# A spectral convolution and spline network: part of the mixing weights loaded among the images, the square root's table loaded in the forward block, the pairs' bias computed behind the first mixing units, and the small loads issued by ScalarE

## The chip, the cores and the metric

The kernel runs on one core of a Trainium2 chip. The metric is the device time of one execution in microseconds (us); lower is better. A core has TensorE (PE, matmuls; its weight loads are shown apart as PEld), VectorE (DVE), ScalarE (ACT), GpSimd (POOL) and SyncE (SP). DMAs are issued by SP, ACT or POOL, each on a queue of its own, and all of them are moved by the core's 16 DMA engines.

## The reference

```python
x: (16, 64, 128, 128) f32          # batch, channels, height, width
xn = group_norm(x)                 # 32 groups of 2 channels, no affine part
# spectral convolution: keep 16 x 16 modes of the lowest and of the highest rows
x_ft = rfft2(xn)
out_ft[:, :, :16, :16]  = einsum('bixy,ioxy->boxy', x_ft[:, :, :16, :16],  w1_r + 1j * w1_i)
out_ft[:, :, -16:, :16] = einsum('bixy,ioxy->boxy', x_ft[:, :, -16:, :16], w2_r + 1j * w2_i)
y = irfft2(out_ft) + conv1x1(xn, conv_w) + conv_b
# two KAN layers on the channels: silu(y) @ base.T + cubic B-splines(y) . (spline * scaler)
y = kan(kan(y, k1), k2)
out = x + gelu(y)
```

Each of w1_r, w1_i, w2_r, w2_i is (64, 64, 16, 16) f32, 4 MB.

## The kernel before

The program has four blocks, one after the other; at the end of a block every engine waits for the others (the branch rows with line 296 stand there).

**Forward block** (`forward`). For each of the 16 images, SP loads eight chunks (`load` inside `forward`, line 362) of 512 KB into `big[:, 0:2]`, which holds two images. PE multiplies two chunks at a time by the DFT table along the height (`h`, line 491: four such stretches per image, h0 to h3, the first needing chunks 0 and 1, the second 2 and 3, and so on), ACT copies the result out of PSUM (line 580), PE turns it (`turn`, line 501), ACT orders it (line 588), and PE does the transform along the width one image late (`w`, line 513). DVE takes the statistics of each chunk (line 430) and keeps the modes (line 421). Chunk k of image b+2 is loaded when PE and DVE are done with chunk k of image b (`next_image`). Image 0 comes first; then DVE's spline weights, which start as soon as eight small loads by POOL's queue (`natural_loaded`) are there, are turned by PE (line 563) while DVE goes on to the statistics; then the images 1 to 15. The last image is followed by the means and variances (lines 538 to 546 on PE, 444 to 455 on DVE). Behind the images' loads SP issues the mixing weights of group 0: w1_r into `big[:, 2]` (eight DMAs of 512 KB, line 160) and the first half of w1_i into `big[:, 3]` (four).

**Mixing block** (`statistics_and_mix`). SP at once loads the rest: the second half of w1_i (whose place held scratch of the forward block), and then w2_r and w2_i over the two images' places; these are 4 + 8 + 8 = 20 DMAs of 512 KB. Meanwhile ACT takes the square root of the variance (line 716), DVE makes the reciprocal `rs_c` (lines 750 to 754) and the pairs' means (757, 758), PE makes the pairs' bias (688), DVE copies it (764, 766), and then the mixing starts. It runs in four passes: group 0 real, group 0 imaginary, group 1 real, group 1 imaginary, each needing its own 4 MB of weights, each of 8 units x; for each unit DVE scales the modes (line 785) and PE does 32 matmuls (705). Behind the second and the fourth pass ACT copies each finished unit (726) and stores it by two DMAs (729). When all are stored, SP loads the modes for the inverse transform.

**Second half** (`second_half`): inverse transform along the height, and then 128 tiles of the inverse along the width, 1x1 convolution and two KAN layers. It fills the rest of the time and no line of the change touches it.

The lines that release PE's first work, before (549 is the head of PE's part):

```python
            pe.wait_ge(tables_loaded, 48)          # dft_h, the identity and dft_w, 16 each
            image(0, 0, 0, before=False)
            pe.wait_ge(mats_ready, 1)
```

## Time and profile before

| | |
|---|---|
| median of 3 runs | 3696.25 us (3695.16 to 3698.87) |
| the profiled execution | 3700.55 us, of which the span shown in the trace is 3698.7 us |
| PE busy | 3629.4 us, 98% of the span |
| DVE, ACT, POOL busy | 3480.8, 3374.5, 116.3 us |
| forward block | 0 to 248.7 us of the span |
| mixing block | 248.7 to about 332 us |
| second half | about 332 us to the end |

The trace shows one execution; times in it count from the start of its span. A row of a timeline has the start, the time from the first to the last instruction of the row, the engine, the line, the operation, the tiles written and read, the count, and in brackets how long the engine sat idle ahead of it and what released it. The DMA share in a window can stand above 1, because packets of one engine overlap.

### The profile page before, as it was taken

To read this page: it belongs to the slowest core of one execution; us is meant where nothing else is said; L and a number is where in the kernel's file an instruction comes from. 1 tells how busy PE (TensorE), PEld (TensorE's weight loads), DVE (VectorE), ACT (ScalarE), POOL (GpSimd) and SP (SyncE) were. 2 spreads that over 40 slices of the span, in tenths; PEclk is the share of its full clock that TensorE was granted. 3 is DMA by queue.
4 is the path that set the end of the run, shared out by engine and by line. 5 is a ranking of instruction groups with operands and counts; after the bars stand their busy time and mean duration, and the time that the engine had idled before them with its cause. 6 is when DMAs were issued, how large, how long until landed. Compare 5 with 4: busy or idle time off the path is not lost.

```text
span 3698.7 us, 98607 instructions
## 1 busy us (share of the span) xinstructions
PE 3629.4 (98%) x36932; PEld 1565.2 (42%) x36932; DVE 3480.8 (94%) x3548; ACT 3374.5 (91%) x3510; POOL 116.3 (3%) x140
## 2 busy tenths in 40 slices
PE   8987999999999999999999999999999999999998
PEld 4555657654333333333333333333333333333333
DVE  8875999999999999999999999999999999999997
ACT  4433999999999999999999999999999999999997
POOL 0000000000000000000000000000000000000000
PEclk9998999999999999999999999999999999999999
DMA  9998243432322323223232232322323222232231
GB/s 320 328 214 200 61 120 89 118 93 60 76 69 65 77 58 76 68 66 77 58 76 67 67 74 60 77 66 68 73 61 77 64 70 71 63 77 64 70 73 50
DMA packets 269760, 338.45 MB, mean 92 GB/s; under 512 B 83272, under 2 KB 198824, under 8 KB 267624
## 3 DMA queue, kind: packets, MB, share of 16 engines
q1 hardware_dynamic: 248392, 265.50, 25.3%
q0 software_dynamic: 18720, 67.49, 10.1%
q10 hardware_dynamic: 2560, 4.20, 0.4%
q8 instruction: 67, 1.10, 0.1%
q14 instruction: 21, 0.17, 0.0%
HBM read 248.50 MB, written 88.61 MB: 91 GB/s over the span
## 4 chain that ended last, share of the span: by engine, by line
PE 90%; SPq 1%; issue 1%; DMA 1%; ACTq 0%; ACT 0%; DVE 0%; DVEq 0%
PE l_ps L1241 84%; PE y_banks L1218 3%; PE y_banks L1227 2%; SPq L160 1%; PE y_banks L1260 1%; PE y_banks L1202 1%; PE y_banks L1189 0%; PE y_banks L1241 0%; DMA big<-in_spec_w_i_dram 0%; ACTq L729 0%; ACT mixed L726 0%; DMA rows_scratch<-rows 0%; PE l_ps L1260 0%; DMA modes_scratch<-mixed 0%; PE mix_ps L705 0%
## 5 line engine op out<-in xcount | busy, mean ns | idle before, releaser
L1121 ACT ACTIVATE offset<-size 128x1024 f32<-128x1024 f32 x1280 | 1241.0, 1045 | 8.1
L1047 DVE SCALAR_TENSOR_TENSOR cube0r<-below,offset 128x1024 f32<-128x1024 f32 x256 | 312.6, 1221 | 113.2 <-ACT offset L1121 103.2
L1047 DVE SCALAR_TENSOR_TENSOR cube2r<-below,offset 128x1024 f32<-128x1024 f32 x256 | 311.5, 1217 | 0.6 <-PE l_ps L1241 0.6
L1047 DVE SCALAR_TENSOR_TENSOR cube0l<-above,offset 128x1024 f32<-128x1024 f32 x256 | 311.7, 1217 | 0.0
L1047 DVE SCALAR_TENSOR_TENSOR cube1r<-below,offset 128x1024 f32<-128x1024 f32 x256 | 311.6, 1217 | 0.0
L1047 DVE SCALAR_TENSOR_TENSOR cube1l<-above,offset 128x1024 f32<-128x1024 f32 x256 | 311.6, 1217 | 0.0
L1047 DVE SCALAR_TENSOR_TENSOR cube3r<-below,offset 128x1024 f32<-128x1024 f32 x256 | 311.5, 1217 | 0.0
L1047 DVE SCALAR_TENSOR_TENSOR cube2l<-above,offset 128x1024 f32<-128x1024 f32 x256 | 311.5, 1217 | 0.0
L1047 DVE SCALAR_TENSOR_TENSOR cube3l<-above,offset 128x1024 f32<-128x1024 f32 x256 | 311.5, 1217 | 0.0
L1047 DVE SCALAR_TENSOR_TENSOR cube4l<-above,offset 128x1024 f32<-128x1024 f32 x256 | 311.4, 1217 | 0.0
L1047 DVE SCALAR_TENSOR_TENSOR cube4r<-below,offset 128x1024 f32<-128x1024 f32 x256 | 311.4, 1216 | 0.0
L1057 DVE SCALAR_TENSOR_TENSOR inner_cube<-below,square 128x1024 f32<-128x1024 f32 x256 | 311.4, 1216 | 0.0
L1241 PE MATMUL l_ps<-S,turned_w 64*64 64x512 f32 x2040 | 280.9, 604 | 10.9 <-issue 10.9
L1117 ACT ACTIVATE size<-below 128x1024 f32<-128x1024 f32 x256 | 270.9, 1058 | 8.1
L1241 PE MATMUL l_ps<-cube0l,turned_w 64*64 64x512 f32 x2040 | 275.5, 590 | 1.7 <-issue 1.7
L1241 PE MATMUL l_ps<-below,turned_w 64*64 64x512 f32 x2040 | 276.6, 593 | 0.4 <-issue 0.4
L1241 PE MATMUL l_ps<-cube2r,turned_w 64*64 64x512 f32 x2040 | 275.5, 589 | 0.5 <-issue 0.5
L1241 PE MATMUL l_ps<-inner_cube,turned_w 64*64 64x512 f32 x2040 | 275.8, 589 | 0.0
L1241 PE MATMUL l_ps<-cube0r,turned_w 64*64 64x512 f32 x2040 | 275.8, 592 | 0.0
L1241 PE MATMUL l_ps<-cube4l,turned_w 64*64 64x512 f32 x2040 | 275.4, 589 | 0.0
L1241 PE MATMUL l_ps<-bowl,turned_w 64*64 64x512 f32 x2040 | 275.4, 589 | 0.0
L1241 PE MATMUL l_ps<-cube4r,turned_w 64*64 64x512 f32 x2040 | 275.4, 589 | 0.0
(169 smaller groups left out, 5963.3 us busy)
## 6 DMA issues: line engine op xcount, KB each, us to landing
big<-in_x_dram SPq DMA_DIRECT2D x128, 512.0 KB, 8.3
x_ring<-in_x_dram SPq DMA_DIRECT2D x256, 256.0 KB, 4.6
out_dram<-act_out SPq DMA_DIRECT2D x128, 512.0 KB, 2.6
act_out<-in_x_dram POOLq DMA_DIRECT2D x127, 512.0 KB, 7.0
rows_t<-rows_scratch SPq DMA_DIRECT2D x512, 32.0 KB
rows_scratch<-rows SPq DMA_DIRECT2D x14, 1024.0 KB, 6.8
pair_t<-pair_scratch SPq DMA_DIRECT2D x128, 65.0 KB, 1.9
big<-in_spec_w_r_dram SPq DMA_DIRECT2D x16, 512.0 KB, 11.6
```

The costliest lines, as they stand in the source:

```text
L160: sp.dma_start(dst[half * C:(half + 1) * C, o0:o0 + MIX_O, :, :], src[:, o0:o0 + MIX_O, x0:x0 + SH, :]).then_inc(t["mix_loaded"][g][part], 16)
L1047: nc.vector.scalar_tensor_tensor(out=cube[q][side][:], in0=distance[own][:], scalar=EDGE - KNOTS[q], in1=offset[own][q][:], op0=ALU.min, o ...
L1057: nc.vector.scalar_tensor_tensor(out=inner_cube[:], in0=below[own][:], scalar=EDGE, in1=square[own][:], op0=ALU.subtract, op1=ALU.mult).th ...
L1117: nc.scalar.activation(size[own][:], below[own][:], ACT.Abs, bias=EDGE, scale=-1.0).then_inc(size_ready[layer], 1)
L1121: nc.scalar.activation(offset[own][q][:], size[own][:], ACT.Square, bias=-KNOTS[q]).then_inc(offset_ready[layer], 1)
L1202: ins = nc.tensor.matmul(y_ps[image, at:at + W], rows[half, par, h, :], inv_w_sb[half, i, :], start=False, stop=(h == HH - 1), skip_group_ ...
L1218: nc.tensor.matmul(y_banks[image, at:at + GW], pair_t[par][half, image], src[half, i * MM + g2 * GW:i * MM + (g2 + 1) * GW], start=True, s ...
L1227: ins = nc.tensor.matmul(y_banks[:, at:at + W], rows[q, par, 2 * e:2 * e + 2, :].rearrange("q i o -> q (i o)"), inv_w4_sb[q, :], start=Fal ...
L1241: ins = nc.tensor.matmul(dst[cols, r * MM:(r + 1) * MM], kan_w[layer][rows_, f, :], src[rows_, n * MM:(n + 1) * MM], start=(f == 0), stop= ...
L1260: ins = nc.tensor.matmul(inv_bank(n, u)[h], inv_h_sb[own, part, h], spec[pair % 2][own, cols:cols + MM], start=True, stop=True, tile_posit ...
```

## The change

Of w1_r, four of the 64 output channels are now loaded after each of the images 2 to 15, as two DMAs of 128 KB (14 times, 56 channels); the last eight channels and the first half of w1_i follow as before. PE's first work waits for the table along the height alone; the other two tables are waited for ahead of the first `turn`. The eight small loads move from POOL's queue to ACT's, ahead of everything else on ACT. A square root of one element, which is used by nobody, stands at the end of ACT's part of the forward block. In the mixing block the pairs' means, PE's bias and its copies move behind DVE's second and fourth unit and PE's second; the bias is written to the PSUM banks of the last two units instead of the third and fourth, and DVE's first pass is written out instead of looped.

```diff
+O_IMAGE = 4
+O_AMONG = O_IMAGE * (B - 2)
+def load_mix_weights_among(sp, t, dst, image):
+    for half in range(2):
+        x0 = SH * half
+        sp.dma_start(dst[half * C:(half + 1) * C, bass.ds((image - 2) * O_IMAGE, O_IMAGE), :, :],
+                     t["w1_r"][:, bass.ds((image - 2) * O_IMAGE, O_IMAGE), x0:x0 + SH, :]).then_inc(t["mix_loaded"][0][0], 16)
...
-            sp.dma_start(dft_h_sb[:], t["dft_h"]).then_inc(tables_loaded, 16)
+            sp.dma_start(dft_h_sb[:], t["dft_h"]).then_inc(dft_h_loaded, 16)
...
                 for par in range(2):
                     next_image(b2, par)
+                    sp.wait_ge(weights_turned, len(TURNS))
+                    load_mix_weights_among(sp, t, weights[:, 2], 2 * b2 + par)
             sp.wait_ge(consts_loaded, 160)
-            sp.wait_ge(weights_turned, len(TURNS))
-            load_mix_weights(sp, t, weights[:, 2], 0, 0, 0, C)
+            load_mix_weights(sp, t, weights[:, 2], 0, 0, O_AMONG, C)
             load_mix_weights(sp, t, weights[:, 3], 0, 1, 0, C // 2)
-        @block.gpsimd
-        def _(pool):
...
-                pool.dma_start(kan["spline"][own], s_).then_inc(natural_loaded, 16)
-                pool.dma_start(kan["scaler"][own], c_).then_inc(natural_loaded, 16)
-                pool.dma_start(kan["mats"][own, F_SILU, :], b_).then_inc(natural_loaded, 16)
-                pool.dma_start(kan["mats"][own, NF, :], t["conv_w"]).then_inc(natural_loaded, 16)
...
                 for k in range(1, N_GRP // 2):
                     h(b, b2, par, k)
+                    if k == 1 and not before:
+                        pe.wait_ge(tables_loaded, 32)
...
-            pe.wait_ge(tables_loaded, 48)
+            pe.wait_ge(dft_h_loaded, 16)
...
+                nc.scalar.dma_start(kan["spline"][own], s_).then_inc(natural_loaded, 16)
+                nc.scalar.dma_start(kan["scaler"][own], c_).then_inc(natural_loaded, 16)
+                nc.scalar.dma_start(kan["mats"][own, F_SILU, :], b_).then_inc(natural_loaded, 16)
+                nc.scalar.dma_start(kan["mats"][own, NF, :], t["conv_w"]).then_inc(natural_loaded, 16)
             act.sem_inc(flat_ready, 4)
             act.sem_inc(freq_ready, 2)
             image(0, 0)
...
+            act.wait_ge(averages_set, 2)
+            nc.scalar.activation(root_of_one, avg[:, 0:1], ACT.Sqrt)
...
-        ps_bias = [ps[2 + i][:, 0:PAIRS] for i in range(2)]
+        ps_bias = [ps[SH - 2 + i][:, 0:PAIRS] for i in range(2)]
...
-                    pe.wait_ge(t["mix_loaded"][g][part], 32 * (C // MIX_O))
+                    pe.wait_ge(t["mix_loaded"][g][part], 32 * (C // MIX_O if g + part else B - 1))
...
+                        if g == 0 and part == 0 and x == 2:
+                            bias()
+                        if g == 0 and part == 0 and x == SH - 2:
+                            pe.wait_ge(bias_kept, 1)
...
+            for x2 in range(SH // 2):
+                for u in range(2):
+                    norm(0, 0, x2, u)
+                if x2 == 0:
+                    means_of_pairs()
+                if x2 == 1:
+                    bias_of_pairs()
```

How it stands on the queues, in the order of each engine's instructions. First SP, from the end of its loop over the images on: `in_x_dram` are the images, `in_spec_w_r_dram` w1_r (and, in the mixing block, w2_r), `in_spec_w_i_dram` w1_i (and w2_i); REGISTER_ALU and COMPARE_AND_BRANCH end the loop, and the two UNCONDITIONAL_BRANCH rows are the way from the forward block to the mixing block. Before:

```order
L362 ISA
L362 DMA big<-in_x_dram 128x4x256
L395 REGISTER_ALU
L395 COMPARE_AND_BRANCH
L160 DMA big<-in_spec_w_r_dram 64x16x128 x8
L160 DMA big<-in_spec_w_i_dram 64x16x128 x4
L296 UNCONDITIONAL_BRANCH
L661 UNCONDITIONAL_BRANCH
L160 DMA big<-in_spec_w_i_dram 64x16x128 x4
L160 DMA big<-in_spec_w_r_dram 64x16x128 x8
L160 DMA big<-in_spec_w_i_dram 64x16x128 x8
```

The same place now (the loop's body, for two images, ends with the first six rows; the pair of weight DMAs stands behind the first image of the body too, and the last w_i row, x8, follows the last row shown):

```order
L160 ISA x2
L160 DMA big<-in_spec_w_r_dram 64x4x128
L160 ISA
L160 DMA big<-in_spec_w_r_dram 64x4x128
L409 REGISTER_ALU
L409 COMPARE_AND_BRANCH
L173 DMA big<-in_spec_w_r_dram 64x8x128 x2
L173 DMA big<-in_spec_w_i_dram 64x16x128 x4
L309 UNCONDITIONAL_BRANCH
L677 UNCONDITIONAL_BRANCH
L173 DMA big<-in_spec_w_i_dram 64x16x128 x4
L173 DMA big<-in_spec_w_r_dram 64x16x128 x8
```

Eight DMAs of 512 KB ahead of the branch have become 28 of 128 KB inside the loop and two of 256 KB behind it; what stands behind the branch is the same twenty as before.

Then ACT at the start of the program, first before and then now (`flat_or_spec<-along_h` is the copy that waits for PE's first stretch, `in_k_...` and `in_conv_w_dram` are the small loads):

```order
L575 UNCONDITIONAL_BRANCH
L580 ACT_TABLE_LOAD
L580 ACTIVATE flat_or_spec<-along_h 128x512 x2
L588 ACTIVATE freq<-planes 128x33x8
L580 ACTIVATE flat_or_spec<-along_h 128x512
```

```order
L582 UNCONDITIONAL_BRANCH
L607 DMA big<-in_k_spline_dram 64x512
L608 DMA big<-in_k_scaler_dram 64x64
L609 DMA big<-in_k_base_dram 64x64
L610 DMA big<-in_conv_w_dram 64x64
L607 DMA big<-in_k_spline_dram 64x512
L608 DMA big<-in_k_scaler_dram 64x64
L609 DMA big<-in_k_base_dram 64x64
L610 DMA big<-in_conv_w_dram 64x64
L587 ACT_TABLE_LOAD
L587 ACTIVATE flat_or_spec<-along_h 128x512 x2
```

Eight DMA issues now stand ahead of ACT's first work, and ahead of its increments of `flat_ready`, for which PE's first stretch waits.

Last, ACT from the end of its loop over the images to its first copy of a mixed unit, first before and then now (`root<-var` is the root that DVE waits for):

```order
L605 COMPARE_AND_BRANCH
L296 UNCONDITIONAL_BRANCH
L713 UNCONDITIONAL_BRANCH
L716 ACT_TABLE_LOAD
L716 ACTIVATE root<-var 128x16
L726 ACTIVATE mixed<-mix_ps 128x512
```

```order
L619 COMPARE_AND_BRANCH
L623 ACT_TABLE_LOAD
L623 ACTIVATE big<-big 128x1
L309 UNCONDITIONAL_BRANCH
L734 UNCONDITIONAL_BRANCH
L737 ACTIVATE root<-var 128x16
L747 ACTIVATE mixed<-mix_ps 128x512
```

The table load has moved from behind the branch to ahead of it, with one more small ACTIVATE.

## Rows read from the trace of the kernel before

**Rows 1.** The page: its span, and the chain that ended last, by engine

```profile
span 3698.7 us, 98607 instructions
...
PE 90%; SPq 1%; issue 1%; DMA 1%; ACTq 0%; ACT 0%; DVE 0%; DVEq 0%
```

**Rows 2.** Windows: length, busy us (instructions) by engine, PEclk, DMA share, GB/s

```profile
40.00:140.00 100.00, 100.00 (x1252) 57.67 (x1254) 87.35 (x259) 49.96 (x117) 0.00 (x0) 1.00 1.09 348
140.00:205.00 65.00, 65.00 (x776) 36.12 (x769) 55.79 (x166) 33.03 (x78) 0.00 (x0) 1.00 0.97 312
210.00:215.00 5.00, 5.00 (x48) 2.44 (x42) 5.00 (x16) 2.64 (x8) 0.00 (x0) 1.00 1.23 184
240.00:249.00 9.00, 6.77 (x52) 2.66 (x46) 5.78 (x11) 0.28 (x1) 0.00 (x0) 1.00 0.46 70
249.00:312.00 63.00, 44.73 (x772) 43.25 (x772) 38.86 (x85) 6.02 (x10) 0.56 (x1) 0.85 1.14 214
```

**Rows 3.** Timeline of PE: first stretches of images 1, 2, 15; last of 2

```profile
29.40 3.66 PE L491 MATMUL along_h<-big,dft_h_sb 64*64 64x512 f32 x32 [1.16 <-ACT turned_w L602]
...
43.10 3.66 PE L491 MATMUL along_h<-big,dft_h_sb 64*64 64x512 f32 x32
...
50.62 1.95 PE L491 MATMUL along_h<-big,dft_h_sb 64*64 64x512 f32 x16
...
221.11 3.66 PE L491 MATMUL along_h<-big,dft_h_sb 64*64 64x512 f32 x32
```

**Rows 4.** Timeline of SP in the forward block, two of its rows

```profile
32.25 172.81 SPq L362 DMA_DIRECT2D big<-in_x_dram  x112
205.31 19.52 SPq L160 DMA_DIRECT2D big<-in_spec_w_r_dram  x8
```

**Rows 5.** Line 362, image loads, from 30 to 62 us

```profile
DMA to landing us min/median/max: 3.9/8.6/9.0
```

**Rows 6.** Waits on SP, from 140 to 180 us: total, times, longest

```profile
SPq L390 <- PE along_h L491: 15.1, 9, 4.3
```

**Rows 7.** Line 160, weight loads, from 249 to 312 us; issue ns min/median/max

```profile
L160 SPq DMA_DIRECT2D big<-in_spec_w_i_dram x12: 595/2654/4190, 248.7 to 300.9; - x12
L160 SPq DMA_DIRECT2D big<-in_spec_w_r_dram x8: 2712/2949/3614, 254.1 to 275.3; - x8
...
DMA to landing us min/median/max: 5.8/12.4/13.1
```

**Rows 8.** Timelines of PE, PEld, DVE at the start of the program

```profile
9.33 6.01 PE L491 MATMUL along_h<-big,dft_h_sb 64*64 64x512 f32 x32 [9.33 <-DMA dft_w_sb<-dft_w_dram]
...
11.06 0.28 PEld L491 LDWEIGHTS along_h<-big,dft_h_sb 64*64 64x64 f32 x4 [0.57 <-issue]
13.10 0.33 PEld L491 LDWEIGHTS along_h<-big,dft_h_sb 64*64 64x64 f32 x8 [1.76 <-issue]
...
11.94 0.69 DVE L241 TENSOR_TENSOR big<-big 128x512 f32<-128x512 f32 x1 [9.58 <-DMA big<-in_conv_w_dram]
...
24.72 3.53 PE L563 MATMUL planes<-eye_all,big 128*64 128x128 f32 x60 [0.58 <-ACT freq L588]
```

**Rows 9.** Timeline of ACT: DMA issues beside SP's full queue

```profile
276.91 1.10 ACTq L729 DMA_DIRECT2D modes_scratch<-mixed  x2
...
290.86 1.94 ACTq L729 DMA_DIRECT2D modes_scratch<-mixed  x2
```

**Rows 10.** Timelines of ACT, DVE and PE in the mixing block

```profile
248.72 1.28 ACT L716 ACT_TABLE_LOAD   x1 [9.80 <-PEq L296]
...
251.47 0.16 DVE L757 COPY pair_mean<-mean_c 64x8 f32<-64x8 f32 x1
...
253.46 0.16 DVE L769 COPY rs_own<-rs_c 64x16 f32<-64x16 f32 x1
...
255.95 14.52 PE L705 MATMUL mix_ps<-big,stats 128*64 128x64 f32 x256 [3.23 <-DVE stats L785]
...
312.05 14.52 PE L705 MATMUL mix_ps<-big,stats 128*64 128x64 f32 x256 [6.95 <-DMA big<-in_spec_w_i_dram]
```

More of the change, by code:

```diff
@@ L157, in load_mix_weights @@
     for o0 in range(o_first, o_end, MIX_O):
+        o1 = min(o0 + MIX_O, o_end)
         for half in range(2):
             x0 = SH * (half if g == 0 else 1 - half)
-            sp.dma_start(dst[half * C:(half + 1) * C, o0:o0 + MIX_O, :, :],
-                         src[:, o0:o0 + MIX_O, x0:x0 + SH, :]).then_inc(t["mix_loaded"][g][part], 16)
+            sp.dma_start(dst[half * C:(half + 1) * C, o0:o1, :, :],
+                         src[:, o0:o1, x0:x0 + SH, :]).then_inc(t["mix_loaded"][g][part], 16)
 def place(j):
@@ L326, in forward @@
             for k in range(3))
+        root_of_one = late[:, at + 7 * n_bg:at + 7 * n_bg + 1]
         flat = [t["flat_or_spec"][:, i * HALF * W:(i + 1) * HALF * W].rearrange("p (f w) -> p f w", w=W) for i in range(2)]
@@ L340, in forward @@
         img_loaded = [[sem(f"img_loaded{p}{k}") for k in range(N_GRP)] for p in range(2)]
-        tables_loaded = sem("tables_loaded")
+        tables_loaded, dft_h_loaded = sem("tables_loaded"), sem("dft_h_loaded")
         along_h_done, flat_ready = sem("along_h_done"), sem("flat_ready")
@@ L684, in _, with bias @@
         def _(pe):
-            pe.wait_ge(rm_ready, 1)
-            for i in range(2):
-                rows = slice(i * C, (i + 1) * C)
-                ins = nc.tensor.matmul(ps_bias[i][rows, :], conv_two[rows], pair_rm[rows, :], start=True, stop=True,
-                                       tile_position=(i * C, i * C))
-            ins.then_inc(bias_done, 1)
+            def bias():
+                pe.wait_ge(rm_ready, 1)
+                for i in range(2):
+                    rows = slice(i * C, (i + 1) * C)
+                    ins = nc.tensor.matmul(ps_bias[i][rows, :], conv_two[rows], pair_rm[rows, :], start=True, stop=True,
+                                           tile_position=(i * C, i * C))
+                ins.then_inc(bias_done, 1)
             pe.sem_inc(mix_done, 2)
@@ L773, in _ @@
                                                 op0=ALU.mult, op1=ALU.add))
-            for g in range(2):
-                for pass_ in range(2):
-                    with dve.Fori(0, SH // 2) as x2:
-                        for u in range(2):
-                            place_ = 2 * x2 + u if g == 0 else x2 * -2 + (SH - u)
-                            dve.wait_ge(mix_done, 2 * x2 + (2 * SH * g + SH * pass_ + u + 1))
-                            here = modes[:, bass.ds(place_, 1), g, :, :].rearrange("p s (k r) b -> p (s k) r b", r=2)
-                            takes = ((0, rs_own), (1, rs_own)) if pass_ == 0 else ((1, rs_neg), (0, rs_own))
-                            for f, (part, scale) in enumerate(takes):
-                                ins = nc.vector.tensor_tensor(
-                                    normed[u][:, :, f, :, :], here[:, :, part:part + 1, :].to_broadcast([P, MODES, 2, B]),
-                                    scale[:].unsqueeze(1).to_broadcast([P, MODES, 2, B]), ALU.mult)
-                            ins.then_inc(normed_ready, 1)
-                    if g == 0 and pass_ == 0:
-                        for b in range(B):
-                            nc.vector.tensor_scalar(pair_all[:, b // 2, b % 2 * C:(b % 2 + 1) * C], conv_two,
-                                                    rs_c[:, b:b + 1], None, ALU.mult).then_inc(pair_made, 1)
@@ new lines, in norm @@
+            def norm(g, pass_, x2, u):
+                place_ = 2 * x2 + u if g == 0 else x2 * -2 + (SH - u)
+                dve.wait_ge(mix_done, 2 * x2 + (2 * SH * g + SH * pass_ + u + 1))
+                here = modes[:, bass.ds(place_, 1), g, :, :].rearrange("p s (k r) b -> p (s k) r b", r=2)
+                takes = ((0, rs_own), (1, rs_own)) if pass_ == 0 else ((1, rs_neg), (0, rs_own))
+                for f, (part, scale) in enumerate(takes):
+                    ins = nc.vector.tensor_tensor(
+                        normed[u][:, :, f, :, :], here[:, :, part:part + 1, :].to_broadcast([P, MODES, 2, B]),
+                        scale[:].unsqueeze(1).to_broadcast([P, MODES, 2, B]), ALU.mult)
+                ins.then_inc(normed_ready, 1)
@@ new lines, in _ @@
+            for x2 in range(SH // 2):
[5 more added lines that the diff above has]
+                    bias_of_pairs()
+            for b in range(B):
+                nc.vector.tensor_scalar(pair_all[:, b // 2, b % 2 * C:(b % 2 + 1) * C], conv_two,
+                                        rs_c[:, b:b + 1], None, ALU.mult).then_inc(pair_made, 1)
+            for g, pass_ in ((0, 1), (1, 0), (1, 1)):
+                with dve.Fori(0, SH // 2) as x2:
+                    for u in range(2):
+                        norm(g, pass_, x2, u)
```

33 lines of the change are left out of this document (18 added, 15 removed).

## The prediction

> **What bounds the kernel now.** I read the page's chain first: PE's own work is 90% of it [rows 1], and nearly all of that is the second half, from about 332 us of the span to its end, whose instructions the change leaves alone. So only the first 332 us can move, and the question is which engine or queue ends each stretch there. 0.2% of this kernel is 7.4 us; that is about what its measurement can tell from no change.
>
> *Forward block.* The timeline of PE shows the beat of the images: image 1 begins at 29.40, image 2 at 43.10, image 15 at 221.11 [rows 3]. From 29.40 to 221.11 are 14 images at 13.69 us, and the one pair of neighbours shown has the same distance (13.70). A queue that fell behind would show as a longer beat; there is none, so PE sets the pace from 29.40 on. The DMA engines are not idle, though: the windows show 348 GB/s at a share of 1.09 until 140 us [rows 2]. An image is 8 x 524,288 B, or 12.05 us at that rate, 1.64 us less than PE's beat. The loads start late, catch up, and by 140 to 180 us SP waits for PE instead (15.1 us in nine waits) [rows 6] and the rate drops to 312 GB/s [rows 2]. That catching up is the spare room that the moved weights will use.
>
> *Mixing block.* SP issues 12 + 8 = 20 weight DMAs between 248.7 and 300.9 us, each taking up to 3 or 4 us because the queue is full, and they land about 12.4 us after issue [rows 7]. PE's fourth pass begins at 312.05 after waiting 6.95 us for the last w_i transfer [rows 10], and everything later hangs on it. Ahead of 249 us the queue had run dry: share 0.46, 70 GB/s [rows 2]. So the stage from 249 to 312 is the time of what is issued behind the block's end, and not of what was left over from before. As a cross-check: pure weight traffic, in runs of 512 B, goes at 184 GB/s [rows 2], so 10.49 MB take 57.0 us; by the page's count of bytes the window moved 13.5 MB in all (63.0 us at 214 GB/s) [rows 2], so the 3 MB more, mostly stores and the pairs' table, took the rest.
>
> **The change, part by part.**
>
> *Weights among the images.* The pair of 128 KB DMAs behind each image is 262,144 B, 1.42 us at 184 GB/s. With the image's 12.05 the queue needs 13.47 us per image against PE's 13.69: it fits by 0.22. Whether it fits from the beginning is a matter of the lead. Image 2's first chunk is issued at 32.25 [rows 4] and lands 3.9 us later (the shortest there, since the queue is empty then) [rows 5], at 36.15; its eighth follows seven chunks of 1.506 us later, at 46.7. PE needs it for its last stretch at 50.62 [rows 3]. The lead is 3.9 us, and the earlier chunks have as much or more. From there it grows by 0.22 per image instead of 1.64: 6.8 us at image 15. PE does not notice; cost 0. Had the lead been nothing and the queue the bound, the 14 pairs would cost 14 x 1.42 = 19.9 us. For the price of a pair I have no row of so small a load among the images. From below it can't be under its bytes at 348 GB/s, 0.75 us; from above, if a 128 KB DMA took the 2.65 us that a 512 KB one holds the queue [rows 7], the pair would be 5.3. I take 1.42, because the transfers overlap and bytes in 512 B runs set the rate [rows 2, 7].
>
> The Trainium skill's page "DMA: Bandwidth & Descriptors", section "Anatomy of one DMA — SWDGE (gpsimd) path", gives a DMA about 2.0 us plus its bytes at 436 GB/s; it would make the pair an estimated 4.6 us if these costs stood one behind the other. Its section "Specifications" says that runs of 512 B already reach the line rate, which would make the pair an estimated 0.75 us. The trace agrees with neither: 512 KB DMAs of 512 B runs follow each other every 2.65 us, at about half the rate of the 1 KB runs of the images. By the first the time would be the slow rival below, by the second nothing changes in the sum.
>
> What does it give? After the last image come the remaining two w_r DMAs of 256 KB and four w_i DMAs: 2.85 + 11.4 us. Image 15's last chunk lands at 221.11 + 7.52 - 6.8 = 221.8, so with its own pair the queue runs dry at about 237.5, some 5 us sooner than before, and then waits for the block's end at 248.7 as it does now. The order of rows shows the same twenty DMAs behind the branch. The gain is 0.
>
> *Root's table.* The load of 1.28 us behind the block's end [rows 10] goes to a time when ACT has sat idle for 9.80 us (same row's bracket) and before the block ends: hidden there. If that cover were gone it would cost 1.28.
>
> *Pairs' bias.* DVE spends 251.47 to 253.46, 1.99 us, on the pairs' means, on waiting for PE and on the copies [rows 10]; with about 1.0 of the table load's 1.28 (VectorE's first small operations overlap the rest) mixing starts 3.0 us earlier, at 252.9 instead of 255.95. Some of it comes back, as DVE does the same work between its units: up to 2 us, inside the first pass. Then the second pass starts up to 3 us earlier, the third waits for its weights instead, and the fourth starts when the last w_i lands, which is 6.95 us after PE was ready already. The wait becomes longer, not shorter: gain 0. On PE the bias stands ahead of the third unit and unit 7 waits for `bias_kept`; behind both are only units of the first pass, which has those 3 us and more to spare.
>
> *The start.* PE's first stretch waits until 9.33 for dft_w; it need now wait for chunk 1 only, which is ahead of the two 64 KB tables in the queue. But weight loads of this stretch follow each other by 0.85 and the next one comes at 13.10 instead of 11.9 [rows 8]: PE waited there a second time, for chunk 3. From then on a pair of chunks lands every 3.0 us, at about 16.1 and 19.1, where PE's next stretches stood at 16.3 and 19.2. So an earlier first stretch only makes PE wait longer at 13.1; I take a gain of 0.1 to 0.2 us. The small loads (360 KB) are moved by the same engines in the same microseconds, whoever issues them; DVE starts its spline weights some 2 to 4 us before 11.94 [rows 8], and what PE waits for at 24.72 is ACT's last copy of image 0, not DVE [rows 8]. At best the 360 KB, 1.0 us at 348 GB/s, fall wholly behind chunk 3: gain 1.0. At worst ACT's eight issues take 0.97 each, as the slowest pair beside a full SP queue did (1.94) [rows 9], so with a start at 1.1 and the table load ACT is free at 10.2, PE starts 0.9 later than 9.33 and the second stretch 0.8 later: loss 0.8. Typical is 0.55 (1.10 the pair) [rows 9], free by 6.8, no loss.
>
> *Sum.* 0 (weights) + 0 (table) + 0 (bias) - 0.15 (start). On the profiled execution, 3700.55 us with its span of 3698.7, that is 3700.4; it was 4.3 above the median of 3696.25, so I put the same difference on the median: 3696.1.
>
> **The rivals.**
>
> *The mixing's head start reaches the end* (chance 0.05). If PE's fourth pass did not hang on the weights, all 3.0 us would arrive, with the start up to 4: 3692 to 3693. Against it stands the wait of 6.95 for a DMA. The Trainium skill's page "ScalarE: Activation LUTs", section "What ACT_TABLE_LOAD costs", prices a switch of tables at about 2.66 us; the row has 1.28. By the page this rival would be an estimated 1.4 us better, and the forecast the same.
>
> *The mixing stage shortens by the bytes that left group 0* (0.04). 3.67 MB at 184 GB/s are 19.9 us: 3676. It would need the queue still to be full at the block's end; it counts from the point where weights of w1_r were late. The share of 0.46 speaks against.
>
> *The queue becomes the bound of the forward block* (0.08; the one on the other side). The place is the wait of PE's stretches on image chunks. The lead of 3.9 is used up by image 15 if a pair costs 3.9 / 13 + 0.22 = 0.52 us more than 1.42, so from about 1.95. At twice its price, 2.84, the loss is 13 x 1.20 - 3.9 = 11.7 us: 3708. At the upper bound of 5.3 it is 13 x 3.66 - 3.9 = 43.7: 3740. Slower by 7.4 begins at a pair of 2.3. For it speaks that the spare is only 0.22 per image; against, that rates here follow bytes and run length.
>
> *ACT's issues hold up the start* (0.06). ACT's increments of `flat_ready` stand behind eight issues. If they took SP's full-queue pace of about 1.5 us each, ACT would be free at 14.4 and the whole beat 4 to 5 us late: 3700 to 3701, still within 0.2%. Beside a full queue they took 0.55 to 0.97 [rows 9].
>
> **How the numbers follow.** The forecast has 0.77. It, the head start and the late ACT are all within 0.2%, nearly 0.88; slower is 0.08, faster 0.04 and a little for what I overlook. The range takes in the bounds of the start (3695 to 3697), the head start at 3692, the late ACT up to 3700, and the spread of runs (3.7 us over three). It leaves out the two rivals beyond 0.2%.
>
> **What would show it.** The beat of PE's L491 stays at 13.69 us with no wait on images; SP no longer waits for PE between 140 and 180 us, and the rate there is near 310 to 330 GB/s with weights among it. The forward block ends at 248.5 or so. The table load stands near 240 on ACT. PE's first mixing matmul comes about 4 us after the block's end instead of 7.2, and the fourth pass still about 63 us after it, with a wait of 7 us or more on w_i. Wrong would be: a beat over 13.69, waits of L491 on `in_x_dram`, a first stretch after 9.33, or a last w_i that lands much sooner than 63 us behind the block's end.

## The result, and the profile after

The changed kernel takes 3702.89 us in the median (22 runs, 3699.27 to 3711.63), the kernel before 3696.12 in the same series (22 runs, 3693.02 to 3705.92): a ratio of 1.0019, 95% interval 1.0012 to 1.0025. It is 6.8 us slower, and outside the range that was predicted (3692 to 3700).

The timeline of PE after the change, first stretch of images 1, 3 and 15 and the last stretch of image 15, then the last matmuls of the forward block and the fourth pass of the mixing (the same places as in [rows 3, 10]):

```profile
28.66 3.66 PE L496 MATMUL along_h<-big,dft_h_sb 64*64 64x512 f32 x32 [1.11 <-ACT turned_w L616]
...
56.05 3.66 PE L496 MATMUL along_h<-big,dft_h_sb 64*64 64x512 f32 x32
...
225.72 3.66 PE L496 MATMUL along_h<-big,dft_h_sb 64*64 64x512 f32 x32
...
234.93 1.95 PE L496 MATMUL along_h<-big,dft_h_sb 64*64 64x512 f32 x16 [1.62 <-issue]
...
251.17 1.90 PE L553 MATMUL along_h<-big 128*128 128x512 f32 x4
...
316.72 14.52 PE L726 MATMUL mix_ps<-big,stats 128*64 128x64 f32 x256 [7.91 <-DMA big<-in_spec_w_i_dram]
```

The last matmuls of the forward block before, and then SP's first row behind the block's end, before and after:

```profile
244.88 1.90 PE L546 MATMUL along_h<-big 128*128 128x512 f32 x4
...
248.72 5.38 SPq L160 DMA_DIRECT2D big<-in_spec_w_i_dram  x4
```

```profile
255.00 5.24 SPq L173 DMA_DIRECT2D big<-in_spec_w_i_dram  x4
```

Image 1 begins 0.74 us earlier than before, image 15 4.61 us later (225.72 against 221.11), the block's end 6.28 us later (255.00 against 248.72), and the fourth pass 4.67 us later (316.72 against 312.05). The beat is 13.69 for two images only; from 56.05 to 225.72 twelve images take 14.14 us each. The waits are small, and the profile puts them down to "issue" (here 1.62) and names no DMA; that they are waits for the images is read from the lengthened beat, from the queue below, and from e1.

The DMA windows after, with the columns of [rows 2]; the second is the dip around one pair of weight loads, the third the stretch behind it, the last lies ahead of the block's end, where the queue has run dry:

```profile
40.00:140.00 100.00, 97.52 (x1209) 56.10 (x1204) 85.58 (x254) 48.35 (x113) 0.00 (x0) 1.00 1.10 315
59.50:63.50 4.00, 4.00 (x36) 2.23 (x32) 4.00 (x13) 1.91 (x5) 0.00 (x0) 1.00 1.12 233
64.00:72.00 8.00, 7.62 (x118) 5.11 (x122) 6.17 (x18) 3.34 (x9) 0.00 (x0) 1.00 1.09 345
140.00:205.00 65.00, 63.55 (x740) 35.59 (x736) 54.36 (x161) 31.18 (x73) 0.00 (x0) 1.00 1.08 317
248.00:256.00 8.00, 5.07 (x8) 1.21 (x6) 4.45 (x12) 0.21 (x1) 0.00 (x0) 1.00 0.00 0
```

Where before there were 348 GB/s from 40 to 140 us [rows 2], there are now 345 in the stretch between two pairs and 233 for four microseconds at the pair, at the same or a higher share of busy engines. These 4 us moved 0.93 MB, 0.26 of them the pair's if all of it falls into them; at 184 GB/s for the pair and 348 for the rest this would have taken 3.35 us (worked out). The forecast had reckoned with 310 to 330 GB/s from 140 to 180 us and took them for a queue that keeps up. There are 317 from 140 to 205 us, but the queue doesn't keep up: SP has no wait on PE or DVE anywhere between 30 and 240 us, where it had 15.1 us of them on PE from 140 to 180 alone [rows 6]. A rate below the full one with no wait of the issuing engine is a queue that is behind.

The second pair on SP's queue, a row of its timeline:

```profile
56.02 2.34 SPq L160 DMA_DIRECT2D big<-in_spec_w_r_dram  x2
```

This pair is issued at 56.02 and the fourteenth at 225.28, so that they follow each other by 14.10 us in the mean. An image alone takes 12.05, so the pair costs 2.05 us, where the sum had 1.42.

### The profile page after: what moved, and what is told of

It is laid out like the page before. It is cut to its first block, busy times and chain, and to the rows that moved or that the text cites. A ratio compares the mean times of both kernels' runs of the same rounds, so it can differ in the third digit from the quotient of the medians.

```text
span 3701.2 us, 98670 instructions
## 1 busy us (share of the span) xinstructions
PE 3627.2 (98%) x36932; PEld 1586.4 (43%) x36932; DVE 3481.1 (94%) x3548; ACT 3374.3 (91%) x3511; POOL 110.4 (3%) x132
## 4 chain that ended last, share of the span: by engine, by line
PE 90%; SPq 1%; DMA 1%; issue 1%; ACTq 0%; ACT 0%; DVE 0%; DVEq 0%
PE l_ps L1275 83%; PE y_banks L1252 3%; PE y_banks L1261 2%; SPq L173 1%; PE y_banks L1294 1%; PE y_banks L1236 1%; PE y_banks L1223 0%; PE y_banks L1275 0%; DMA big<-in_spec_w_i_dram 0%; ACTq L750 0%; ACT mixed L747 0%; DMA rows_scratch<-rows 0%; PE l_ps L1294 0%; DMA rows_t<-rows_scratch 0%; DMA modes_scratch<-mixed 0%
## 5 line engine op out<-in xcount | busy, mean ns | idle before, releaser
L1275 PE MATMUL l_ps<-cube3l,turned_w 64*64 64x512 f32 x2040 | 277.3, 589 | 0.0
```

Source lines behind the costliest of these rows:

```text
L1275: ins = nc.tensor.matmul(dst[cols, r * MM:(r + 1) * MM], kan_w[layer][rows_, f, :], src[rows_, n * MM:(n + 1) * MM], start=(f == 0), stop= ...
```

## The experiments

The table takes the start of image 1, the beat (mean of the images from 3 on), the start of the fourth pass and PE's wait ahead of it from each kernel's one trace. The difference of medians is against the kernel before on the same chip, in whose own trace the fourth pass begins at 312.05 [rows 10].

| kernel | image 1 | beat | fourth pass (wait) | time, and less before | ratio (95%) |
|---|---|---|---|---|---|
| changed kernel | 28.66 | 14.14 | 316.72 (7.91) | 3702.89, +6.8 | 1.0019 (1.0012 to 1.0025) |
| e1_no_among | 28.45 | 13.69 | 310.60 (8.98) | 3698.08, +2.0 | 1.0004 (0.9995 to 1.0013) |
| e2_among_only | 29.79 | 14.2 | 319.43 (8.95) | 3703.34, +7.3 | 1.0024 (1.0014 to 1.0035) |
| e3_every_second | 30.09 | 14.0 | 316.97 (8.69) | 3703.33, +7.3 | 1.0021 (1.0012 to 1.0031) |
| e4_long_runs | 29.02 | 13.69 | 312.44 (9.40) | 3701.63, +5.6 | 1.0017 (1.0008 to 1.0026) |
| e5_all_partitions | 28.57 | 13.69 | 310.73 (8.86) | 3696.90, -0.9 | 0.9994 (0.9984 to 1.0004) |
| e6_table_bias | 29.33 | 13.69 | 311.69 (9.00) | 3696.71, -1.1 | 0.9996 (0.9987 to 1.0005) |
| e7_early | 30.45 | 13.69 | 304.56 (4.86) | 3693.47, -4.3 | 0.9985 (0.9976 to 0.9994) |
| e8_two_early | 28.79 | 13.69 | 302.66 (0.43) | 3686.91, -10.9 | 0.9968 (0.9956 to 0.9980) |
| e9_three_early | 28.73 | 13.69 | about 305.7 (none) | 3692.22, -4.9 | 0.9987 (0.9977 to 0.9996) |
| e10_start | 29.52 | 13.69 | 311.31 (8.21) | 3697.72, +0.6 | 1.0000 (0.9991 to 1.0009) |
| e11_two_early16 | 29.94 | 13.69 | 306.42 (5.83) | 3693.42, -3.3 | 0.9992 (0.9983 to 1.0001) |
| e12_two | 30.10 | 13.69 | 311.51 (8.48) | 3699.05, +2.3 | 1.0004 (0.9995 to 1.0013) |

The fourth pass is the sharper reading of the first 320 us. From its start to GpSimd's first load for the tiles of the second half all kernels take 86 to 89 us; but single early tile steps differ between the traces by up to 5 us (below), and the differences of the medians lie up to 5 us off those of the fourth pass.

**Which part costs: e1 and e2.** e1_no_among is the changed kernel without the weights among the images; e2_among_only is the kernel before with them alone.

```diff
-                    sp.wait_ge(weights_turned, len(TURNS))
-                    load_mix_weights_among(sp, t, weights[:, 2], 2 * b2 + par)
...
+            sp.wait_ge(weights_turned, len(TURNS))
...
-            load_mix_weights(sp, t, weights[:, 2], 0, 0, O_AMONG, C)
+            load_mix_weights(sp, t, weights[:, 2], 0, 0, 0, C)
```

> The changed kernel with only the loading of w1_r among the images undone (all eight 512 KB DMAs behind the last image again). Theory A (the pair of weight DMAs behind each image costs the queue about 2.1 us instead of 1.42, so the queue sets the beat of the images): the beat of PE's first stretches goes back from 14.10 to 13.69 us, image 1 still begins at 28.66 (0.74 earlier than before), the forward block ends 0.7 us earlier than before the change, the mixing stage keeps its gain of about 1 us; time 3694 to 3695.5. Rival B (the loss sits in the other parts: small loads by ScalarE, bias, table): the beat may be 13.69 but the time stays over 3700.

> The kernel before with only the loading of w1_r among the images added. Theory A: image 1 begins at 29.40 as before, the beat is about 14.1 us, the forward block ends 5 to 6 us later than before, and so does the fourth mixing pass; time 3701 to 3703. Rival B: 3696, as before. Rival C (the beat is slow since the start came 0.74 us earlier and ate the lead): the beat is 13.69 for the first images and the end comes under 3 us later.

Without the loads among the images the beat is 13.69 and the fourth pass begins at 310.60; with them alone the beat is 14.2 and it begins at 319.43. The loss is theirs, and the other parts are no cause of it. e1's median lies 2.0 above before while its fourth pass is 1.45 earlier: its interval takes in a ratio of 1.

**What makes a pair dear: e3, e4, e5.** Three ways of moving the same 3.67 MB among the images. e3_every_second loads eight channels behind every second image (14 DMAs of 256 KB). e4_long_runs takes runs of 2 KB instead of 512 B in the same pairs; e5_all_partitions takes one DMA of 256 KB over all 128 partitions, in runs of 512 B as before. In e4 and e5 other weights land in these places than the mixing needs, so the output is not the reference's.

```diff
# e3
+        sp.dma_start(dst[half * C:(half + 1) * C, bass.ds((image - 1) * 2 * O_IMAGE, 2 * O_IMAGE), :, :],
+                     t["w1_r"][:, bass.ds((image - 1) * 2 * O_IMAGE, 2 * O_IMAGE), x0:x0 + SH, :]).then_inc(t["mix_loaded"][0][0], 16)
...
-                    load_mix_weights_among(sp, t, weights[:, 2], 2 * b2 + par)
+                load_mix_weights_among(sp, t, weights[:, 2], b2)
# e4
+        run = O_IMAGE * SH * MODES
+        sp.dma_start(dst[half * C:(half + 1) * C].rearrange("p o x k -> p (o x k)")[:, bass.ds((image - 2) * run, run)],
+                     t["w1_r"].rearrange("c o x k -> c (o x k)")[:, bass.ds((image - 2) * run, run)])\
+          .then_inc(t["mix_loaded"][0][0], 16)
# e5
+    src = t["w1_r"].rearrange("c (s o) x k -> (c s) o (x k)", s=2)
+    sp.dma_start(dst[:, bass.ds((image - 2) * O_IMAGE, O_IMAGE), :, :].rearrange("p o x k -> p o (x k)"),
+                 src[:, bass.ds(image - 2, O_IMAGE), 0:SH * MODES]).then_inc(t["mix_loaded"][0][0], 16)
```

> The changed kernel with eight channels behind every second image instead of four behind each: the same bytes in 14 DMAs of 256 KB instead of 28 of 128 KB. Theory A1 (a fixed cost of about 0.33 us per DMA on top of its bytes makes the pair dear): the two 256 KB DMAs cost 2 x (0.35 + 1.4) = 3.5 us per two images, 1.75 per image, so the beat is 13.8 and the forward block ends 3.5 to 4 us earlier than in the changed kernel; time about 3698.5. Theory A2 (transfers to half of the partitions get in the way of the images' transfers for as long as bytes of theirs are in the queue, by bytes): the beat stays at 14.0 to 14.1, time 3702 to 3703. Theory A3 (each switch from one kind to the other costs): half as many switches, the beat 13.75.

> The changed kernel with the 28 DMAs among the images reading contiguous runs of 2 KB instead of four runs of 512 B (same count, same bytes, same 64 partitions; the weights that land are not those of the reference). Theory L (short runs of 512 B set the rate of 184 GB/s): a pair costs at most 0.75 us and a little, the queue is no bound, the beat is 13.69, time about 3695. Theory P (writing to only 64 of the 128 partitions sets the rate, whatever the runs): the pair costs 1.4 to 2.1 as now, the beat 14.0 to 14.1, time 3702 to 3703.

> The changed kernel with one DMA of 256 KB behind each image instead of two of 128 KB: the same bytes in the same number of 512 B runs, but written to all 128 partitions (the weights that land are not those of the reference). The run with 2 KB runs in the same 64 partitions left the beat at 13.69, so run length matters. Theory R (the number of 512 B runs alone makes the load dear among the images, about 2.1 us for 512 runs): the beat stays near 14.1 and the fourth mixing pass starts near 316 to 317. Theory RP (short runs and half of the partitions together; each engine pair then writes one port): with all partitions the load costs 0.8 to 1.4 us, the beat is 13.69 and the fourth pass starts near 311 to 312.

The window from 60 to 100 us of e5:

```profile
60.00:100.00 40.00, 40.00 (x492) 22.82 (x494) 34.66 (x103) 20.36 (x48) 0.00 (x0) 1.00 1.10 343
```

The price of the loads per image is the mean distance of the weight issues, from the second to the fourteenth, less 12.05:

| bytes per image, form | distance | price |
|---|---|---|
| 262,144 in two DMAs, 64 partitions each, 512 B runs (changed kernel) | 14.10 | 2.05 |
| the same, 2 KB runs (e4) | 13.73 | 1.68 |
| the same bytes in one DMA, 128 partitions, 512 B runs (e5) | 12.96 | 0.91 |
| 131,072 in two DMAs, 64 partitions each, 512 B runs (e12, e11, e8) | 12.96, 13.02, 13.11 | 0.91 to 1.06 |
| 196,608, the same form (e9) | 13.72 | 1.67 |

(In none of these kernels does SP wait for PE or DVE between 30 us and the last pair, so the distance is the queue's own, and not PE's beat. The changed kernel's form cost 2.19 in e2 and in e3, so a price is good to some 0.15.) e3 has half as many weight DMAs of twice the size, and its weight issues lie 14.24 us apart per image (from 81.43 to 223.87 for ten images) all the same: neither the number of DMAs nor the change from images to weights and back is what is paid for.

Longer runs take off 0.37. The 128 partitions take off 1.14, with the short runs kept: the larger part of the price goes with writes that reach 64 partitions only. e3 shows that e5's gain is not that of one large DMA in place of two small ones. One thing was not held fixed: e4 and e5 read other addresses of w1_r than the pair does, some of them several times, and no run tries that alone.

The Trainium skill's page "SBUF — State Buffer", section "Door 1: The DMA port swizzle (why `[64,N]` ≈ `[32,N]`)", says that partitions 0 to 63 reach only 8 of the 16 ports by which DMAs write, and 64 to 127 the other 8; the two DMAs of a pair write one half each. The trace agrees in size: 184 GB/s for weights alone [rows 2] and 343 GB/s with e5's form among the images, most of which are the images' own bytes. Which ports were used no run here shows.

**Table and bias: e6.** The kernel before with root's table in the forward block and the pairs' bias behind the first units.

```diff
+            act.wait_ge(averages_set, 2)
+            nc.scalar.activation(root_of_one, avg[:, 0:1], ACT.Sqrt)
...
-        ps_bias = [ps[2 + i][:, 0:PAIRS] for i in range(2)]
+        ps_bias = [ps[SH - 2 + i][:, 0:PAIRS] for i in range(2)]
...
+                        if g == 0 and part == 0 and x == 2:
+                            bias()
```

> The kernel before with only the root's table in the forward block and the pairs' bias behind the first units; start and weights as before. By the chain nothing of it arrives at the end, since the fourth mixing pass waits for the last weights: its start within 0.5 us of 312, the wait for it longer by 2 to 3 us; time 3696, at most 0.5 off. Rival (one of these parts costs something later, as the run without the weights among the images hints, which came out 2 us above before though its fourth pass began 1.45 us earlier): 3698 to 3700.

The first and the fourth pass of e6:

```profile
252.66 3.80 PE L726 MATMUL mix_ps<-big,stats 128*64 128x64 f32 x64 [5.96 <-DVE stats L808]
...
311.69 13.52 PE L726 MATMUL mix_ps<-big,stats 128*64 128x64 f32 x238 [9.00 <-DMA big<-in_spec_w_i_dram]
```

The mixing begins 3.29 us earlier than before (252.66 against 255.95), and the fourth pass waits 9.00 instead of 6.95 [rows 10] and begins 0.36 earlier. The head start becomes a wait.

**The start: e10.** The kernel before with one part of the start changed: the first stretch waits for dft_h alone, the turns for the other tables; the small loads stay on POOL's queue.

```diff
-            pe.wait_ge(tables_loaded, 48)
+            pe.wait_ge(dft_h_loaded, 16)
...
+                    if k == 1 and not before:
+                        pe.wait_ge(tables_loaded, 32)
```

> The kernel before with one part of the change: the first stretch of TensorE waits for dft_h alone, the turns for the other two tables; the small loads stay on GpSimd's queue. Theory: this wait is all of the 0.7 us that the start gained, so the first stretch begins near 8.0 (before 9.33), image 1 near 28.7, and the fourth pass near 311.3, no measurable difference in the time (3696). Rival (the small loads on ScalarE's queue gave the start): image 1 stays at 29.4. A third possibility: TensorE stands idle for 0.6 us or more between the first two stretches, the clock does not rise for the second, and image 1 comes at 30.0 or later.

PE's second stretch of e10, then its first two of the changed kernel and of e7 (the same start as the changed kernel):

```profile
13.29 1.95 PE L491 MATMUL along_h<-big,dft_h_sb 64*64 64x512 f32 x16 [1.81 <-DMA big<-in_x_dram]
```

```profile
8.00 3.69 PE L496 MATMUL along_h<-big,dft_h_sb 64*64 64x512 f32 x16 [8.00 <-DMA big<-in_x_dram]
12.29 1.95 PE L496 MATMUL along_h<-big,dft_h_sb 64*64 64x512 f32 x16 [0.59 <-issue]
```

```profile
7.68 3.69 PE L499 MATMUL along_h<-big,dft_h_sb 64*64 64x512 f32 x16 [7.68 <-DMA big<-in_x_dram]
12.14 3.69 PE L499 MATMUL along_h<-big,dft_h_sb 64*64 64x512 f32 x16 [0.77 <-DMA big<-in_x_dram]
```

The wait for dft_h alone gives nothing: the second stretch then stands 1.81 us for chunk 3, and image 1 begins at 29.52 (before 29.40). So the theory fell, and its rival, that the small loads' move gave the 0.7, is what is left; the move without the other wait was not tried. The third possibility fell as well: PE stood idle for 1.81 us ahead of a second stretch that took 1.95. With the loads on POOL's queue the DMA engines move 217 GB/s from 9 to 11 us (210 before), with them on ACT's 331, and chunk 3 lands at 12.20 instead of 13.20 (13.04 before). DVE's spline weights start no earlier by it: 12.04 against 11.94 [rows 8].

In e7, and likewise in e3, e11 and e12, the second stretch began at 11.85 to 12.14 instead of 12.20 or later and took 3.69 us instead of 1.95 to 2.12, so that image 1 came at 29.9 to 30.5: later than before the change. In the ten traces with the changed start image 1 comes six times 0.4 to 1.0 us earlier than in the kernel before and four times 0.5 to 1.1 later, with the mean 0.1 earlier.

**Fewer channels per image: e12.** The changed kernel with `O_IMAGE = 2`: 28 of 64 channels among the images, 36 behind them.

> The changed kernel with two channels per image among the images instead of four, and nothing loaded earlier than that: 28 of 64 channels of w1_r, the other 36 by five pairs behind the loop. Theory (the price of a pair, 1.1 us for two channels, is under the spare of 1.64 that the queue has per image without loads): the beat is 13.69, the last image's loads come no later, the queue begins the rest some 10 us earlier than without loads among the images, and the fourth pass begins at 308 to 309 against 310.6; the time is 3695 to 3697, not measurably different from before. Rival (any load among the images puts the last image's data late, however small): the beat is above 13.69, and the time is at least 3699.

The beat is 13.69, as the theory said: 1.0 us is under the spare of 1.64. But the fourth pass begins at 311.51, not at 308 to 309. Its image 1 comes late (30.10 against 28.45), and its block ends at 249.39 where e1's ends at 247.76; but even from the block's end on it gains only 0.7 us on e1 (62.1 against 62.8). The window from 236 to 252 us, of e12 and then of e7:

```profile
236.00:252.00 16.00, 10.97 (x89) 4.87 (x87) 9.77 (x24) 2.50 (x5) 0.00 (x0) 1.00 0.09 20
```

```profile
236.00:252.00 16.00, 11.33 (x89) 4.86 (x87) 9.15 (x19) 2.50 (x5) 0.00 (x0) 1.00 1.23 190
```

The queue has nothing left that it may load before the block's end: 20 GB/s where e1, without loads among the images, has 111. What was loaded early only makes this hole longer. Even with a beat that holds, weights of w1_r among the images buy nothing by themselves.

**Filling the hole: e7, e8, e9, e11.** e7 is e1 with the first 32 channels of w2_r (four DMAs of 512 KB) loaded into image 14's place as soon as PE and DVE are done with it. e8 has two channels per image and 48 channels early, e9 three and 48, e11 two and 16.

```diff
+EARLY = 32
...
             load_mix_weights(sp, t, weights[:, 3], 0, 1, 0, C // 2)
+            sp.wait_ge(along_h_done, N_GRP // 2 * (B - 1))
+            sp.wait_ge(stats_ready, N_GRP * (B - 1))
+            load_mix_weights(sp, t, weights[:, 0], 1, 0, 0, EARLY)
...
-                load_mix_weights(sp, t, mix_w[1][part], 1, part, 0, C)
+                load_mix_weights(sp, t, mix_w[1][part], 1, part, 0 if part else EARLY, C)
```

> The changed kernel without the loads among the images, and with four of the eight w2_r DMAs (32 of 64 channels) issued at the end of the forward block, as soon as PE and DVE are done with image 14, whose place they take; 16 DMAs instead of 20 stay behind the block's end. The queue, which runs dry some 7 us ahead of the block's end, is kept full. Theory: the fourth pass starts 6 to 7 us earlier than in the kernel without this (310.60), at 303.5 to 305, and the time is 3690 to 3692. Rival: the early loads delay the second pass's w1_i by more than its slack, or the block's end, and nothing is gained (3696 to 3698).

> The changed kernel with two channels of w1_r behind each image instead of four, and six of the eight w2_r DMAs issued at the end of the forward block as soon as image 14's place is free; 14 DMAs stay behind the block's end. Two channels are 256 runs of 512 B: at the measured 2.1 us for 512 of them about 1.05 us, under the 1.64 that the queue has to spare per image, so the beat is 13.69. The fourth pass starts at about 298 to 300, now bound by PE's third pass; time 3684 to 3688. Rival (any weights among the images cost more than their share, by the switch and not by the run): the beat is over 13.8 and the time 3690 or more.

> Three channels per image among the images (42 of 64), and the first 48 channels of w2_r by three pairs behind image 14 instead of in the mixing stage. Theory (the price of the loads grows with their bytes: 1.1 us for two channels per image, 2.1 for four, so some 1.55 for three, under the queue's spare of 1.64 per image): the beat stays 13.69, only two pairs of w_r follow the images, SP's early issue ends near 247 instead of 252, so that the block's end is not held up, and the fourth pass begins near 298 to 300 with almost no wait; the time is some 3682 to 3685. Rival (the lead runs out within the 14 images because a pair costs more than 1.9): the beat is above 13.69 in the last images, the fourth pass begins at 301 or later, and the time is 3687 or more. A second rival: the weights that still come late (w_i) are what the fourth pass waits for, whatever was moved ahead, and it begins at 302 as with two channels.

> Two channels per image among the images, and only the first 16 channels of w2_r (one pair) behind image 14, where the run before had 48. Theory (the end of the forward block was held up because SyncE had not issued its last loads): the early issue now ends near 242, the mixing begins near 252.5 instead of 256.9, the same bytes are in the queue at the same times, so the fourth pass still begins at 302 to 303, now with a wait of some 3 us instead of 0.4: the time is the same as with 48 channels (3687) within its scatter. Rival (the end of the block, and with it the chain of the mixing, sets the fourth pass): it begins near 299, and the time is 3683.

e7 gains 4.3 us with none among the images, and that with image 1 late (30.45). SP's early issues and the mixing of e8 (first rows of each):

```profile
236.10 16.09 SPq L174 DMA_DIRECT2D big<-in_spec_w_r_dram  x6
```

```profile
256.88 3.82 PE L730 MATMUL mix_ps<-big,stats 128*64 128x64 f32 x64 [10.72 <-DVE stats L812]
...
302.66 14.49 PE L730 MATMUL mix_ps<-big,stats 128*64 128x64 f32 x256 [0.43 <-DMA big<-in_spec_w_i_dram]
```

e8 is the best of all: 0.9968 of before (six runs, of which the one traced is the slowest), and its fourth pass waits 0.43 us. Its limit is visible in the first row: SP is held by its own full queue until 252.2, the engines wait for SP at the block's end, and the mixing begins 4 us later than e6's. e9 should have mended that and didn't: with three channels the beat still holds, but at 13.72 us per image against 13.11 its queue comes to the last pair 7.3 us later than e8's (219.38 against 212.05), more than the one pair of 512 KB DMAs less behind the images gives back. SP's early issues run from 238.50 to 255.7, the mixing begins at 260.38, the passes then follow without a wait and the fourth begins near 305.7 (worked out: the last three passes are one row of 43.11 us from 276.99, a third is 14.4). Its last w_i lands at 304.9, so an earlier mixing alone would have given less than 1 us. Both the theory and the rivals had it otherwise.

e11 has SP free early and the mixing at 253.27, but the fourth pass waits 5.83 us and begins at 306.42, later than theory and rival had it and than e7's; its image 1 also comes late (29.94).

What sets the fourth pass is seen when it is counted from the block's end, which is where SP issues the rest:

| kernel | block's end | DMAs of 512 KB behind it | from there to the fourth pass | GB/s from 236 to 252 us |
|---|---|---|---|---|
| kernel before | 248.72 | 20 | 63.3 | 109 |
| changed kernel | 255.00 | 20 | 61.7 | 104 |
| e1_no_among | 247.76 | 20 | 62.8 | 111 |
| e12_two | 249.39 | 20 | 62.1 | 20 |
| e11_two_early16 | 249.25 | 18 | 57.2 | 108 |
| e7_early | 250.20 | 16 | 54.4 | 190 |
| e8_two_early | 252.85 | 14 | 49.8 | 190 |
| e9_three_early | 256.36 | 14 | 49.3 | 191 |

All the kernels with twenty take 61.7 to 63.7 us, and each two DMAs fewer take off some 3 to 6. The bytes moved ahead of the block's end do not decide it by themselves: e12 with 20 GB/s and e1 with 111 take nearly the same, and e11 with e1's rate takes 5.6 less. What counts is how many DMAs are left behind the block's end, and whether SP's own issues delay that end. How much of e8's lead over e7 comes from the two channels per image, and how much from 48 early channels in place of 32, no run separates: none has 48 early and nothing among the images.

## Why the prediction was wrong, by its own steps

**The step that failed** is the price of the pair, and with it the lead (below). The price: "I take 1.42, because the transfers overlap and bytes in 512 B runs set the rate". Measured it is 2.05 us (2.19 in e2 and in e3). The mechanism of the loss stood in the prediction as the rival "The queue becomes the bound of the forward block" (0.08), with 1.95 as the price from which the lead is used up; only the size of the term put it there. The 184 GB/s were read rightly [rows 2]; the reason given for them, the runs of 512 B, is the smaller part. Every row of that traffic has 64 partitions and 512 B runs at once, so the trace of before could not tell them apart; e4 and e5 did, and the partitions are the larger part. And even the right 184 GB/s is a price for weights alone. Mixed among images, the pair costs more than its own 1.42: the dip of 233 GB/s lasts 4 us, where both rates one after the other would give 3.35.

The rival's own arithmetic had a slip: by its formula a loss of 7.4 us begins at a pair of 2.5 us ((7.4 + 3.9) / 13 + 1.64), not 2.3. At 2.05 the formula gives 13 x 0.41 - 3.9 = 1.4 us, so the price alone does not make the loss.

**The lead** was mis-sized too. The sum took the first chunk's landing (3.9) plus seven of 1.506, which puts the eighth at 46.7. The rows of line 362 from 36 to 40 us, in the kernel before, have the eighth issued at 39.6 and these landing after 8.3 us at least:

```profile
L362 SPq DMA_DIRECT2D big<-in_x_dram x3: 372/941/1520, 36.3 to 39.6; - x3
...
DMA to landing us min/median/max: 8.3/8.5/8.7
```

That is 47.9 to 48.3, a lead of 2.3 to 2.7 us and not 3.9. With 2.05 a pair, 13 pairs are 13 x 0.41 = 5.3 us over the spare; the image 15 of the changed kernel is 225.72 - 28.66 - 14 x 13.69 = 5.4 us late, so in effect no lead was left. It went in one step: the eighth chunk of image 3 lands at 64.3, 16.3 us behind image 2's, and PE's beat would have needed it at 63.6. Part of that step is not the pair's, for without loads among the images the same step is 12.7 to 13.3 us in the kernel before, e1, e6 and e10 (12.0 in e7, whose start was late), where the sum had 12.05.

The last stretch of image 15 waits 1.62 more. That is 7.0, less 0.74 from the start: the forward block's last matmul stands at 251.17 where it stood at 244.88, 6.3 later, and so does the block's end. The twenty DMAs behind it then took 1.6 us less than before (61.7 against 63.3 to the fourth pass), so that 4.67 reach the fourth pass. The table and the bias are not shown to have given this back: e6 with both takes 63.0, e10 with neither 62.5, and all kernels with twenty lie between 61.7 and 63.7.

**The rest held.** The loads among the images give nothing behind the loop, since the queue runs dry and waits for the block's end (e12: 20 GB/s there). Table and bias are 0 within the noise, with a head start of 3.0 predicted and 3.29 measured and a wait for w_i that grows instead (e6). The table load is hidden, in ACT's idle time ahead of the block's end (245.24, 1.28 us long). ACT's issues took about 0.6 each and held nothing up.

**The start** was put at -0.15; it is a gain or a loss of about 0.7 by execution, so the mean of -0.1 is near the forecast by luck. The reason given, that an earlier first stretch only makes PE wait longer for chunk 3, is what e10 shows; what was missed is that chunk 3 lands a microsecond sooner once the small loads are on ACT's queue.

**Open.** The medians say +6.8 for the changed kernel and +7.3 for e2, the fourth pass +4.67 and +7.4. The remaining 2 us of the changed kernel are not explained, nor are the 5 of e4, whose fourth pass is only 0.4 later than before and whose interval (1.0008 to 1.0026) lies above 1. Each kernel has one trace, and its executions differ: the two traced ones are only 2.45 us apart (3703.00 and 3700.55). One place where traces differ is a tile step of the second half: between the fourteenth and the fifteenth pair of GpSimd's loads the kernel before shows 31.2 us, the changed kernel 26.7, e10 26.3, e8 31.6. What decides this step, and whether it makes e4's 5 us, was not tried. e4's queue, at 13.73 us per image, is also just at PE's beat, and other executions may fall behind it; no trace shows one.

## What to carry to other kernels

A price read from pure traffic is not the price among other traffic: before moving a load into the spare of a busy queue, ask how many partitions it writes: here the same bytes cost 2.05 us over 64 at a time and 0.91 over 128, and even 1.42, the price of the pure traffic, was too low. Loading earlier helps only if fewer loads stand behind the next barrier; find the window ahead of it in which the queue runs dry and move loads from behind the barrier into that one first (e7: -4.3 us, where the changed kernel lost 6.8). And an engine that issues DMAs into a full queue comes late to the block's end, as SP did in e8 and e9.

## What was not expected of the hardware

- 262,144 B per image over 64 partitions at a time cost 2.05 us, over 128 partitions 0.91, in runs of 512 B both; runs of 2 KB over 64 partitions 1.68. Half as many DMAs of twice the size cost no less (2.19).
- Sixteen matmuls of the second stretch take 3.69 us when they begin at 11.85 to 12.14 and 1.95 to 2.12 when they begin at 12.20 or later, with the granted clock shown as 1.00 in both. PE's idle time ahead of them doesn't sort them: 0.69 to 0.87 us ahead of those of 3.69 us, 0.50 to 1.81 ahead of the others. No run here tells what decides it.
- With the small loads on POOL's queue all traffic from 9 to 11 us is 210 to 218 GB/s, with the same loads on ACT's 321 to 331.
- SP's six early DMAs of 512 KB in e8 took 16.1 us to issue (236.10 to 252.2), since the queue was full, and the block ended at 252.85 where e1's ended at 247.76.
